# Attention with relative positions: the loads of queries, keys, positional keys and values issued by ScalarE in place of SyncE

## The reference

```python
x = x + 0.5 * ffn(layernorm(x))
# attention: H = 16 heads of dh = 16, S = 1024
xn = layernorm(layernorm(x)) * ln_g + ln_b
q, k, v = (xn @ Wq + bq), (xn @ Wk + bk), (xn @ Wv + bv)      # per head [S, 16]
p = pe @ Wp                                                   # positional keys [S, 16] per head
content = einsum("bihd,bjhd->bhij", q + u_bias, k)
pos = relative_shift(einsum("bihd,jhd->bhij", q + v_bias, p))
attn = softmax((content + pos) * dh ** -0.5)
x = x + (attn @ v) @ Wo + bo
x = x + 0.5 * ffn(layernorm(x))
```

## Time and profile before

| | us |
|---|---|
| median of 3 runs | 3663.93 |
| the profiled execution | 3663.37 |
| its span, first to last instruction | 3661.5 |
| TensorE busy | 3358.0 (92%) |
| ScalarE busy | 2309.2 (63%) |
| VectorE busy | 1813.9 (50%) |
| GpSimd busy | 1241.6 (34%) |

### The profile page before, as it was taken

The page is one execution under the profiler, slowest core; times in us unless marked ns, Lnnn a source line. Parts: engine busy times, 40 slices in busy tenths (PEclk is TensorE's granted clock), DMA queues, the critical chain, the costliest instruction groups (busy, mean ns, idle before and its releaser), DMA issues. The chain is left out here.

```text
span 3661.5 us, 85875 instructions
## 1 busy us (share of the span) xinstructions
PE 3358.0 (92%) x24380; PEld 1840.6 (50%) x24380; DVE 1813.9 (50%) x3600; ACT 2309.2 (63%) x3252; POOL 1241.6 (34%) x1212
## 2 busy tenths in 40 slices
PE   4996999999999999999999999999999999999776
PEld 3663444444444444444444444444444444444565
DVE  4872444444444444444444444444444444444444
ACT  1443666667766767676767676766676766676222
POOL 1110333333333333333333333333333333333100
PEclk8997999999999999999999999999999999999888
DMA  3555999999999999999999999999999999999443
GB/s 111 179 185 198 365 370 375 375 375 374 372 374 376 378 373 378 374 372 373 373 372 378 375 372 374 377 377 375 374 372 372 375 375 374 375 373 383 132 103 92
DMA packets 468102, 1221.73 MB, mean 334 GB/s; under 512 B 92256, under 2 KB 176736, under 8 KB 468064
## 3 DMA queue, kind: packets, MB, share of 16 engines
q1 hardware_dynamic: 468064, 1221.26, 92.1%
HBM read 624.38 MB, written 596.65 MB: 333 GB/s over the span
## 5 line engine op out<-in xcount | busy, mean ns | idle before, releaser
L805 DVE CUSTOM_DVE_ANT_0 at_pos_in<-at_ps_con,at_pos_in 128x1024 f32<-128x1024 f32 x1024 | 1254.0, 1225 | 1580.2 <-PE at_ps_con L693 1435.2
L842 POOL TENSOR_SCALAR at_pos_in<-at_pos_in,at_neg_max 128x1024 f32<-128x1024 f32 x1024 | 1145.5, 1119 | 1903.4 <-DVE at_neg_max L805 1903.4
L773 ACT ACTIVATE at_pos_out<-at_ps_pos 128x1024 f32<-128x1024 f32 x1024 | 1048.8, 1024 | 599.1 <-PE at_ps_pos L693 599.1
L782 ACT ACTIVATE at_prob<-at_ps_turn 128x512 f32<-128x512 f32 x2048 | 1110.7, 596 | 362.7 <-PE at_ps_turn L716 362.7
L693 PE MATMUL at_ps_con<-at_right,at_left 32*128 32x512 f32 x4096 | 1156.1, 640 | 149.7 <-DVE at_neg_max L805 148.5
L716 PEld LDWEIGHTS at_ps_turn<-keep_ident,at_pos_in 128*128 128x128 f32 x8192 | 898.8, 143 | 625.8 <-issue 426.8
L693 PE MATMUL at_ps_pos<-at_right,at_left 32*128 32x512 f32 x4096 | 1163.6, 644 | 25.9 <-DMA at_right<-scratch_pos_rows 18.0
L716 PE MATMUL at_ps_turn<-keep_ident,at_pos_in 128*128 128x128 f32 x8192 | 1113.7, 279 | 0.6
L728 PE MATMUL at_ps_pv<-at_prob,at_v_aug 128*32 128x512 f32 x4096 | 545.3, 605 | 0.8 <-issue 0.8
L693 PEld LDWEIGHTS at_ps_con<-at_right,at_left 32*128 32x128 f32 x4096 | 308.0, 183 | 340.8 <-ACT at_pos_out L773 200.7
L739 PEld LDWEIGHTS at_ps_head<-keep_fold,at_head_T 128*128 128x128 f32 x2048 | 247.8, 191 | 195.7 <-DVE at_head_T L813 148.6
(11 more groups left out here) (85 smaller groups left out, 1328.8 us busy)
## 6 DMA issues: line engine op xcount, KB each, us to landing
scratch_scores<-at_pos_out SPq DMA_DIRECT2D x1024, 512.0 KB, 7.6
at_pos_in<-scratch_scores SPq DMA_DIRECT2D x1024, 512.0 KB, 7.7
at_left<-scratch_qk_rows SPq DMA_DIRECT2D x512, 64.0 KB, 5.3
scratch_qk_rows<-de_qk SPq DMA_DIRECT2D x48, 512.0 KB, 5.7
de_x<-in_L_attn_x_dram SPq DMA_DIRECT2D x16, 512.0 KB, 4.7
scratch_x<-de_x_bo SPq DMA_DIRECT2D x16, 512.0 KB, 3.2
scratch_values<-de_values SPq DMA_DIRECT2D x8, 1024.0 KB, 5.1
at_right<-scratch_pos_rows SPq DMA_DIRECT2D x256, 32.0 KB, 5.8
```

The source lines that it names most:

```text
L773: act.activation(pos_out[:, t.slot, :], ps_pos[:, :, :].rearrange("p a m -> p (a m)"), ACT.Copy)\
L782: act.activation(prob[t.t // QUAD % 2][:, 4 * n:4 * n + 4, k * P:(k + 1) * P], ps_turn[:, n, :].rearrange("p (j i) -> p j i", i=P), ACT.Exp)\
L805: dve.tensor_tensor_reduce(pos_in[:, t.slot, :], ps_con[:, :, :].rearrange("p a m -> p (a m)"), pos_in[:, t.slot, :], -SCALE, 3.0e38, ALU. ...
L842: pool.tensor_scalar(pos_in[:, t.slot, :], pos_in[:, t.slot, :], -1.0, neg_max[:, t.slot:t.slot + 1], ALU.mult, ALU.add).then_inc(shifted, 1)
```

## The change

ScalarE's block gets `load_qv` and `load_qk`, word for word with `act` in place of `sp`. `load_qv` stands between `copy_positional` and `exponentials` in the steps t % 8 = 0, `load_qk` behind `exponentials` in the steps t % 8 = 1. The loads before the loop go to the head of ScalarE's block. SyncE keeps `write`, `read_back` and `store_head`.

```diff
         @block.sync
-            def rows_of(name, u): ...
-            def load_qv(u): ...
-            def load_qk(u): ...
@@
             def step(r, t):
                 w = Tile(r, t + LEAD)
                 if w.real():
-                    if w.i == 0 and Tile(r, t + LEAD + TILES).real():
-                        load_qv(Tile(r, t + LEAD + TILES))
                     write(w)
                 back = Tile(r, t + LEAD - READ_LAG)
                 if back.real():
                     read_back(back)
-                if t % TILES == 1 and Tile(r, t - 1 + TILES).real():
-                    load_qk(Tile(r, t - 1 + TILES))
@@
-            sp.wait_ge(blanked, 1)
-            load_qv(Tile(0, 0))
-            load_qv(Tile(0, TILES))
-            load_qk(Tile(0, 0))
@@
         @block.scalar
+            def load_qv(u):
+                if u.past(BODY):
+                    at_once(act, pos_mm, u.units(TILES, -TILES))
+                h, _ = u.head_batch()
+                for n, first in enumerate((2 * STRIP, 3 * STRIP)):
+                    act.dma_start(left[u.side][first:first + STRIP:2, :], rows_of("q_v", u)).then_inc(qv_in[u.side], 16)
+                    act.dma_start(right[u.side][first:first + STRIP:2, :],
+                                 a["pos_rows"][bass.ds(h * DH, DH), n * HALF:(n + 1) * HALF])\
+                        .then_inc(qv_in[u.side], 16)
+
+            def load_qk(u):
+                if u.past(BODY):
+                    at_once(act, con_mm, u.units(TILES, -TILES))
+                    at_once(act, v_ready, u.units(1, -1))
+                for n, first in enumerate((0, STRIP)):
+                    act.dma_start(left[u.side][first:first + STRIP:2, :], rows_of("q_u", u)).then_inc(qk_in[u.side], 16)
+                    act.dma_start(right[u.side][first:first + STRIP:2, :], rows_of("k", u)[:, n * HALF:(n + 1) * HALF])\
+                        .then_inc(qk_in[u.side], 16)
+                h, b = u.head_batch()
+                act.dma_start(v_in[u.side][:, :], a["values"][h * B + b, :, :]).then_inc(vals_in[u.side], 16)
@@
             def step(r, t):
                 if Tile(r, t + LEAD).real():
                     copy_positional(Tile(r, t + LEAD))
+                    if t % TILES == 0 and Tile(r, t + LEAD + TILES).real():
+                        load_qv(Tile(r, t + LEAD + TILES))
                 if Tile(r, t - 1).real():
                     exponentials(Tile(r, t - 1))
-
+                if t % TILES == 1 and Tile(r, t - 1 + TILES).real():
+                    load_qk(Tile(r, t - 1 + TILES))
+
+            act.wait_ge(blanked, 1)
+            load_qv(Tile(0, 0))
+            load_qv(Tile(0, TILES))
+            load_qk(Tile(0, 0))
             for t in range(LEAD):
                 copy_positional(Tile(0, t))
             rounds(act, step)
```

More of the change, by code:

```diff
@@ L611, in _ @@
         def _(sp):
[L612 to L635, removed]
             def write(w):
@@ L768, in _, with rows_of @@
         def _(act):
+            def rows_of(name, u):
+                h, b = u.head_batch()
+                return a["qk_rows"][{"q_u": 0, "q_v": 1, "k": 2}[name], b, bass.ds(h * DH, DH), :]
+            def load_qv(u):
[15 more added lines that the diff above has]
+                        .then_inc(qk_in[u.side], 16)
+                h, b = u.head_batch()
+                act.dma_start(v_in[u.side][:, :], a["values"][h * B + b, :, :]).then_inc(vals_in[u.side], 16)
             def copy_positional(t):
```

## The result

The changed kernel takes **4202.74 us** (4197.33 to 4212.18, 4 runs), the kernel before 3666.36 in the same session. The ratio is 1.147 (95% interval 1.144 to 1.149): 14.7% slower. The forecast was 3966 us with a range up to 4110. The direction was right and the size was not: the loss is 536 us, and 303 were forecast.

What follows compares the result with a forecast made beforehand. TensorE's matmul stream was taken to set the pace, transfers hidden. Late copies behind ScalarE's load batches cost 296 us, SyncE's relief gives back 5, meeting issues add 12: 3663.4 + 296 - 5 + 12 = 3966 us, range 3850 to 4110.

Steps and rivals of the forecast that it cites:

- The rival in which the sequencer runs ahead: ScalarE's load_qk begins at 1511.8 while the exponentials of t wait in the queue; 0.72 us lost a unit, 3760 us; chance 0.07.
- the one of no loss: ScalarE's issues are short enough to lie in its idle time, leaving only SyncE's relief; 3650 us; chance 0.05.
- the price of an issue: ScalarE's loads cost what SyncE's did: in even units 3.20 us for load_qv and 3.95 for load_qk, arithmetic included.
- The rival of dear issues: ScalarE's issues exclude SyncE's or are slower; each 0.1 us per issue adds 113 us, 0.2 gives 4190; chance 0.14.
- The first delay is contained in it: Even unit: load_qv's delay adds nothing to the 2.55 us that the strips of t+3 lose behind load_qk.
- the bullet on the copy of t+9: Even unit: behind load_qv this copy ends at 1513.7, so the strips of t+2 start at 1513.8 instead of 1513.06.
- the banks of the transposes: Late exponentials free the banks late, so the second half of tile t's transposes starts about 0.28 us late.
- the clock: TensorE's granted clock might fall in the attention from pauses of 2 us; left out, as today's pauses leave it at 1.00.
- the net 7 for relief and for meeting SyncE: SyncE's earlier writes and reads save 5 us; ScalarE's issues meeting SyncE's cost 12 us.

Runs made afterwards that it cites:

- e2: Against the changed kernel, load_qv goes back to SyncE, so only load_qk is issued by ScalarE; 4117.13 us, 1.121 of the kernel before.
- e9: The changed kernel with both halves of TensorE's product with the values one step later; 4105.59 us, 1.117 of the kernel before.
- e1: Against the changed kernel, load_qk goes back to SyncE, so only load_qv is issued by ScalarE; 3886.8 us, 1.059 of the kernel before.
- e3: The changed kernel with load_qv moved behind the exponentials of the same step; 3994.63 us, 1.088 of the kernel before.
- e5: The changed kernel with load_qv and two of load_qk's five loads (second keys, values) back on SyncE; 3819.11 us, 1.040 of the kernel before.
- e6: Changed kernel with ScalarE's nine loads spread singly over steps 0 to 4 and the product with the values cut into four pieces; 3577.04 us, 0.974 of the kernel before.
- e11: Kernel before with the product with the values in four pieces; SyncE issues all, loads two by two in steps 0 to 3, values in step 4; 3659.59 us, 0.995.
- e4: The changed kernel with ScalarE's nine loads of a unit issued one by one over steps 0 to 4; 3667.42 us, 0.9994 of the kernel before.

## Why the prediction was wrong

**Right:** that TensorE's stream sets the pace, and the mechanism. ScalarE's sequencer does not get past an activation that waits; the loads begin where the copy or the second exponential is released, and the next activation stands behind the last load (ScalarE's timeline above: 1526.63 to 1529.96). The rival in which the sequencer runs ahead, 3760 us, and the one of no loss are out (measured 4202.74).

**Right in the mean: the price of an issue.** From first to last the batches took 2.88 and 3.25 us on ScalarE, and 2.74 and 3.36 on SyncE before. The rival of dear issues would need some 0.2 us more for each, and it is out as the cause of the miss. The mean hides one place: in even units the batch of four took 3.16 us (2.71 on SyncE before), and in odd units 2.60. The last issue of the even batch is the dear one, 1.33 us in the row at 1491.53. In e2 and e9 the batch of five was dearer by 0.08 us an issue. Why some issues are dearer stays open.

**The step that failed:** "The first delay is contained in it", and ahead of it the bullet on the copy of t+9, which priced `load_qv` by what waits for that copy (0.74 us) and by the banks of the transposes (0.28). It overlooked what else waits for the late exponentials. In step t+1 TensorE's product with the values (L728) takes the exponentials of four tiles, the last of them tile t-1, which ends at 1510.72 in the earlier trace rows, a third of a microsecond ahead of it. This is the product in the kernel before:

```profile
1511.04 1.07 PE L728 MATMUL at_ps_pv<-at_prob,at_v_aug 128*32 128x512 f32 x8
```

With `load_qv` before them the exponentials end at 1512.7, and the product comes at 1512.83 in place of 1511.04: 1.79 us, by the working of the prediction itself, and everything behind it, the release of `load_qk` too, shifts by as much. So the two stalls add up in place of one containing the other. Redone with this edge, the working gives 1.79 + 2.26 in the even unit and 1.58 + 2.01 in the odd: 7.64 us a body. The trace has 7.47 at full clock: 2.24 + 2.08 in the even unit and 1.39 + 1.78 in the odd. That the sums agree so well is in part luck. The even unit's first stall is 0.45 us longer than the working gives, as its batch of four is, and the other three are 0.2 shorter each. e1 shows the first stall alone (3.55 us a body with its 10 falls), e3 shows that it goes with the place of `load_qv` and not with the number of issues, and e9 that it is the exponentials that are waited for.

**The second omission:** the clock. The prediction named it as what would make it wrong and put it at nothing, since the pauses of before, 0.7 us at most, left it at 1.00. Stalls of 2.0 to 3.0 us brought falls (e2, 117 behind 121 stalls); in e3 and e5, where none was longer than 1.6 us, there was none. In the changed kernel it is 66 us.

**The account:** 303 forecast, less the net 7 for relief and for meeting SyncE, 296; the steps t+1, 3.63 us a body in place of the 1.3 that the copy alone would give, 147; the steps t+2 by the rest of 7.47 - 4.61, 0.5 a body, 33; the clock 66. Together 542; measured 536.

## What to carry to other kernels

Before work is put in front of an instruction, list every reader of what that instruction makes, on every engine and in the next step too, and add the delays where one hands on to the next; the reader with the least slack here was 0.3 us away and in no row that was quoted. On an engine whose activations wait for others, put DMA issues one at a time into the gaps behind instructions that are already released: the same nine loads cost 536 us in two batches and nothing when spread. Relieving a queue is worth nothing until it is the bound: with TensorE's step shortened first, spreading the loads to ScalarE gave 2.6%, and either edit alone gave nothing. That fits the Trainium skill ("DMA: Bandwidth & Descriptors", Issuing engines are not separate DMA queues), by which a second issuing engine saves only the sequencer's time: here e6 takes 3577 us and e11, in which SyncE issues all, 3660, though the second queue is not ruled out as a part of that.

## What the runs showed of the hardware

- TensorE resumed at full clock after a stall of 2.71 us and fell to half 1.2 us later, for 3.4 us, in the midst of full work (e2, rows above). Where no stall was longer than 1.6 us the granted clock stayed at 1.00 (e3, e5), but in e9, with second stalls of some 1.9 us, 11 of 56 falls came behind a first stall of 1.4 to 1.6 us.
- An issue on ScalarE's sequencer took 0.54 and 0.55 us while an activation ran beside it (rows of e4), and the activation was not slowed: the copy took 1.02 us as before.
- ScalarE's issues of one and the same line were not all alike: the last of the even unit's batch of four took up to 1.33 us (row at 1491.53), and one in the odd unit 0.75 (row at 1522.21).
- Two queues, one for SyncE and one for ScalarE, cost nothing in themselves: e4 has the time of the kernel before.
